# Cross attention 0: the negated maxima put into the score banks by VectorE in place of a second pair of matmuls

## The chip, the cores and the metric

One core of one Trainium2 chip runs the whole program: a stack of twelve layers over 1024 tokens of width 128. The metric is device time in microseconds (us) of one execution. The kernel before takes 5865.0 us (median of 3 runs, 5858.02 to 5866.67). Only the second layer, cross attention 0, is changed, apart from two constants that nothing used.

## The reference

The layer computes, for 16 heads of size 64, with 1024 queries from the layer's normalised input and about 6,400 keys from a shared context (51 tiles of 128 keys):

```
qw = (q_in @ Wq + bq).reshape(B, M, HEADS, QSIZE)
kw = (k_in @ Wk + bk).reshape(B, N, HEADS, QSIZE)
vw = (v_in @ Wv + bv).reshape(B, N, HEADS, KSIZE)
a = jnp.einsum('bmhd,bnhd->bhmn', qw, kw) / jnp.sqrt(jnp.float32(QSIZE))
a = jnp.where(key_mask[:, None, None, :], a, -jnp.inf)
a = jax.nn.softmax(a, axis=-1)
o = jnp.einsum('bhmn,bnhd->bmhd', a, vw).reshape(B, M, HEADS * KSIZE)
return o @ Wo + bo
```

The softmax takes off a maximum for each query and head before the exponential. Any number near the true maximum will do, as long as it is the same for all keys of that query.

## The kernel before

The 16 heads are taken as 8 pairs (`P`); one head of a pair lies on partitions 0 to 63, the other on 64 to 127. The keys come in 13 chunks of up to 512 (`C`), that is 51 tiles of 128 keys (`KT`); the last chunk has 3 tiles, and its maxima are 260 keys wide. The program is a list of turns `g`; a turn has 4 steps `s` (3 where the chunk scored has 3 tiles). In turn `g` the approximate maxima of chunk `g` are found, and 14 turns later (`LAG = C + 1`) the exact scores of the same chunk are made, chunk `j = g - LAG`. So in the long middle of the layer, turns 14 to 103, every step holds one key tile of scores and two of the eight maxima (`q`) of a later chunk; the last pair's scores have no maxima beside them.

The order on each engine is written out by hand. A step on TensorE: bf16 maxima `q` (line 2310) into banks 4 and 5; scores of query half 0 into banks 0 and 1; scores of half 1 into banks 2 and 3; the second maxima; the products of the previous tile's probabilities with the values (line 2342). In step 0 of a turn the keys and values of the next chunk (lines 2349 and 2354) come between, and that step's second maxima go to bank 0 instead of bank 4. Once a pair each, in other steps: the queries (line 2360), the rows (line 2368, which turn the maxima found by VectorE into a row for each query), the sums (line 2377), the output (line 2384). `take_banks` makes TensorE wait until whoever read a bank last is done.

Scores of one half are two float32 matmuls, one a head (line 2323, 64 partitions of keys against 512 queries), and two bf16 matmuls of a tile of ones with `Qa`, the negated maxima (line 2325), added on in the same banks:

```
nc.tensor.matmul(ps[:, 2 * half + a, :], lhsT=Kr[...], rhs=Q[...], start=True, stop=False)
mm = nc.tensor.matmul(ps[:, 2 * half + a, :], lhsT=ones[head(a), :], rhs=Qa[...], start=False, stop=True)
```

ScalarE takes the exponential of each half (line 2433) and copies keys, values and rows out of PSUM. GpSimd adds the probabilities of all tiles up for the softmax sums (lines 2579 and 2588), one addition for each half; its sums hold back ScalarE, which has four buffers of probabilities. VectorE takes the maximum of each block of maxima scores (line 2521), in turn order: two a step. It also does, once a pair, eight reciprocals (2508), a product (2537), the query scaling (2528), the residual addition (2543) and, at the end of a turn with `g % C == 12`, the small steps from maxima to rows (2561 to 2564). No DMA runs in this stretch.

Of the kernel before, what the change touches and what calls it, by code (L numbers as in the profile page):

```python
# [16 lines left out]
D = 128  # L17
# [2200 lines left out]
def cross_0(k, io, X, stack):  # L2218
# [17 lines left out]
    folding, copied, folded = k("folding", "maxima_copied", "maxima_folded")  # L2236
# [8 lines left out]
    Qa, ones = k.tile(stack, "Qa", [128, 2, S], BF16), k.tile(stack, "ones", [128, 128], BF16)  # L2245
# [7 lines left out]
    mz = k.tile(stack, "mz", [128, 8, 2, 64], BF16)  # L2253
# [22 lines left out]
    def others_at(g, s):  # L2276
        return [(item, p) for item, p in ((item, pair_for(g, s, turn, step)) for item, turn, step in
                (("queries", -1, 1), ("rows", C, 1), ("sums", LAG + C, 1), ("output", LAG + C + 2, 2))) if p is not None]
# [9 lines left out]
    def pair_for(g, s, turn, step):  # L2288

        p = (g - turn) // C  # L2290
        return p if s == step and (g - turn) % C == 0 and 0 <= p < P else None

    def pe():
# [8 lines left out]
        def maxima(i, s, steps, q):  # L2302
            b = maxima_bank(i, s, steps, q)
            take_banks(b, taken_off(i, q))
            if q == 0:
                nc.tensor.wait_ge(*key_copied.at(i + 1))
                nc.tensor.wait_ge(*query_copied.at(i // C + 1))
            n = ctx.keys_in(i % C)
            for a in range(2):
                mm = nc.tensor.matmul(ps[:, b + a, 0:n], lhsT=Qb[head(a), i // C % 2, q * 128:(q + 1) * 128], rhs=Kb[head(a), i % 2, 0:n], start=True, stop=True)  # L2310
            mm.then_inc(*maxima_mm.up())

        def scores(j, s, half):
            t, p = KT * (j // C) + TPC * (j % C) + s, j // C
            if s == 0 and half == 0:
                nc.tensor.wait_ge(*key_set.at(j + 1))
                if j % C == 0:
                    nc.tensor.wait_ge(*query_set.at(p + 1))
                    nc.tensor.wait_ge(*rows_set.at(p + 1))
# [25 lines left out]
        def keys_and_values(i, j):  # L2345
            take_banks(4, *([key_copied.at(i + 1)] if i < N else []), *([value_set.at(j + 1)] if 0 <= j < N else []))
            if i < N:
                p, c = i // C, i % C
                nc.tensor.matmul(ps[:, 4, :], lhsT=wk[:, p * 128:(p + 1) * 128], rhs=masked[:, c * CHUNK:(c + 1) * CHUNK], start=True, stop=True).then_inc(*key_mm.up())
            if 0 <= j < N:  # L2350
# [12 lines left out]
        def rows(p):  # L2363
            take_banks(4, rows_set.at(p + 1))
            nc.tensor.wait_ge(*rows_step.at(3 * p + 3))
# [21 lines left out]
        nc.tensor.wait_ge(*zeroed.at(2))  # L2387
# [6 lines left out]
        for g, j, steps in turns():  # L2394
            for s in range(steps):
# [3 lines left out]
                last = [q for q in items[1:] if g >= LAG and maxima_bank(g, s, steps, q) == 0]  # L2399
# [10 lines left out]
                if s == 0:  # L2410
                    keys_and_values(g + 1, j + 1)
                elif not others and g >= LAG:
                    for q in between:
                        maxima(g, s, steps, q)
                for item, p in others:
                    {"queries": queries, "rows": rows, "sums": sums, "output": output}[item](p)
                for q in last:
                    maxima(g, s, steps, q)
                if 0 <= j and 0 < t <= KT * P and (j < N or s == 0):
                    products(t - 1)  # L2420

    def act():
# [14 lines left out]
        for g, j, steps in turns():  # L2437
            for s in range(steps):
# [31 lines left out]
                p = pair_for(g, s, C, 1)  # L2470
                if p is not None:
                    nc.scalar.wait_ge(*rows_mm.at(p + 1))
                    if p >= 2:
                        nc.scalar.wait_ge(*scored.at(2 * KT * (p - 1)))
                    nc.scalar.copy(Qa[:, p % 2, :], pair).then_inc(*rows_set.up())
                p = pair_for(g, s, LAG + C, 1)
                if p is not None:
# [3 lines left out]
                    nc.scalar.copy(over[:], pair).then_inc(*sums_set.up())  # L2481

    def dve():
        nc.vector.memset(ones[:], 1.0)
        nc.vector.memset(ones_f[:], 1.0)
        nc.vector.memset(zero_row[:], 0.0).then_inc(*zeroed.up())
        nc.vector.memset(mz[:], 0.0).then_inc(*zeroed.up())
# [21 lines left out]

        for g, j, steps in turns():  # L2510
            for s in range(steps):
                for q in maxima_at(g, s, steps):
                    if g < C and q in by_act:
                        waiting.append((g, q))
                        if len(waiting) > 2:
                            fold(*waiting.pop(0))
                        continue
                    nc.vector.wait_ge(*maxima_mm.at(8 * g + q + 1))
                    if g >= 2 * C and g % C == 0 and q == 0:
                        nc.vector.wait_ge(*rows_step.at(3 * (g // C) - 4))  # L2520
                    nc.vector.tensor_reduce(red[:, g // C % 2, q, :, g % C], ps[:, maxima_bank(g, s, steps, q):maxima_bank(g, s, steps, q) + 2, 0:ctx.keys_in(g % C)], AX, ALU.max).then_inc(*reduced.up())  # L2521
                p = pair_for(g, s, -1, 1)
                if p is not None:
# [4 lines left out]
                    nc.vector.tensor_scalar(Q[:, p % 3, :], both.rearrange("p a n -> p (a n)"), bq[:, p:p + 1], scale, ALU.add, ALU.mult).then_inc(*query_set.up())  # L2528
                for n in range(8):
# [8 lines left out]
                p = pair_for(g, s, LAG + C + 2, 2)  # L2538
                if p is not None:
                    nc.vector.wait_ge(*out_mm.at(p + 1))  # L2540
                    if p:
                        nc.vector.wait_ge(*x_added.at(p))
                        nc.vector.tensor_tensor(X[:], X[:], both.rearrange("p a n -> p (a n)"), ALU.add).then_inc(*x_added.up())
                    else:
                        nc.vector.wait_ge(*constant_set.at(1))
                        nc.vector.scalar_tensor_tensor(X[:], both.rearrange("p a n -> p (a n)"), out_bias[:, 0:1], X[:], ALU.add, ALU.add).then_inc(*x_added.up())
            if 0 <= g < N and g % C == C - 1:
# [10 lines left out]
                if p:  # L2558
                    nc.vector.wait_ge(*rows_step.at(3 * p))
                    nc.vector.wait_ge(*rows_mm.at(p))  # L2560
# [815 lines left out]
class Constants:  # L3376
    def __init__(self, k, stack):
# [4 lines left out]
        self.zero = k.tile(stack, "zero", [1, HALF])  # L3382
        self.roots = k.tile(stack, "roots", [128, 8])
        self.ones, self.ones_col, self.ones16 = k.tile(stack, "ones", [1, 128]), k.tile(stack, "ones_col", [128, 1]), k.tile(stack, "ones16", [128, 16])
        self.ident16, self.below16 = k.tile(stack, "ident16", [128, 128], BF16), k.tile(stack, "below16", [128, 128], BF16)
        self.causal, self.below = k.tile(stack, "causal", [128, 128]), k.tile(stack, "below", [128, 128])
        for t, value in ((self.mean, 1.0 / D), (self.eps, LN_EPS), (self.one_eps, 1.0 + 1e-6), (self.zero, 0.0),
                         (self.ones, 1.0), (self.ones_col, 1.0), (self.ones16, 1.0)):
            nc.vector.memset(t[:], value)
        nc.gpsimd.memset(self.ident[:], 0.0)  # L3390
        nc.gpsimd.memset(self.causal[:], 1.0)
# [4 lines left out]
        nc.gpsimd.affine_select(out=self.causal[:], in_=self.causal[:], compare_op=ALU.is_ge, fill=0.0, base=0,  # L3396
                                pattern=[[1, 128]], channel_multiplier=-1)
# [147 lines left out]
```

## Time and profile before

| | |
|---|---|
| median of 3 runs | 5865.0 us |
| the profiled execution: span | 5863.6 us |
| its own time beside the span | none is shown apart from the span |
| busy in the span: TensorE, VectorE, ScalarE, GpSimd | 5274.1, 2726.8, 3176.0, 2218.6 us |
| the changed layer, first to last exponential | 410.3 to 2503.1 us |
| exponentials in it (line 2433) | 816 of 1114 ns |

A line of a view names the source line, the engine, the operation, its output and input, and how often. Busy times of TensorE are of pipelined matmuls: the distance between the starts of two of them says more than the length of one. In a timeline the bracket gives the idle time before an instruction and what ended it.

### The profile page before, as it was taken

To read this page: it belongs to the slowest core of one execution; us is meant where nothing else is said; L and a number is where in the kernel's file an instruction comes from. 1 tells how busy PE (TensorE), PEld (TensorE's weight loads), DVE (VectorE), ACT (ScalarE), POOL (GpSimd) and SP (SyncE) were. 2 spreads that over 40 slices of the span, in tenths; PEclk is the share of its full clock that TensorE was granted. 3 is DMA by queue.
4 is the path that set the end of the run, shared out by engine and by line. 5 is a ranking of instruction groups with operands and counts; after the bars stand their busy time and mean duration, and the time that the engine had idled before them with its cause. 6 is when DMAs were issued, how large, how long until landed. Compare 5 with 4: busy or idle time off the path is not lost. (4 is left out here: it accounts for less than half of the span.)

```text
span 5863.6 us, 69367 instructions
## 1 busy us (share of the span) xinstructions
PE 5274.1 (90%) x28014; PEld 1717.5 (29%) x28014; DVE 2726.8 (47%) x3143; ACT 3176.0 (54%) x3203; POOL 2218.6 (38%) x1113
## 2 busy tenths in 40 slices
PE   8879999999999999989999689999886788888889
PEld 3213333333333333332243311111342111111123
DVE  5664545454545552015541400000246998898713
ACT  4455555555555555521122399999124677777761
POOL 1119898989888899915533000000000000000000
PEclk8869999999999999989999799999896799999999
DMA  1000000000000000010000120000203000000010
GB/s 50 15 1 1 1 1 1 1 1 1 1 1 1 1 1 1 1 41 1 2 1 4 52 84 11 20 11 2 80 25 123 13 11 11 11 11 11 7 46 31
DMA packets 64433, 100.77 MB, mean 17 GB/s; under 512 B 9846, under 2 KB 49880, under 8 KB 62000
## 3 DMA queue, kind: packets, MB, share of 16 engines
q1 hardware_dynamic: 63906, 95.50, 4.9%
q8 instruction: 222, 3.64, 0.3%
q14 instruction: 99, 0.81, 0.0%
q10 hardware_dynamic: 206, 0.83, 0.0%
HBM read 70.85 MB, written 25.31 MB: 16 GB/s over the span
## 5 line engine op out<-in xcount | busy, mean ns | idle before, releaser
L2433 ACT ACTIVATE Pr<-ps,key_bias 128x1024 f32<-128x1024 f32 x816 | 893.2, 1114 | 1015.4 <-PE ps L2325 1015.4
L2521 DVE TENSOR_REDUCE red<-ps 128x2 f32<-128x1024 f32 (+1 forms) x767 | 908.1, 1185 | 959.2 <-PE ps L2310 954.0
L2579 POOL TENSOR_TENSOR Ps<-Ps,Pr 128x1024 f32<-128x1024 f32 x400 | 944.3, 2361 | 215.9 <-ACT Pr L2433 215.9
L2588 POOL TENSOR_TENSOR Ps<-Ps,Pr 128x1024 f32<-128x1024 f32 x400 | 947.5, 2369 | 0.0
L3206 DVE TENSOR_REDUCE red<-ps 128x1 f32<-128x512 f32 (+3 forms) x1024 | 877.7, 908 | 94.0 <-PE ps L3079 74.7
L3162 ACT ACTIVATE Pr<-ps 128x1024 f32<-128x1024 f32 x816 | 786.2, 1021 | 228.5 <-PE ps L3089 227.9
L2323 PE MATMUL ps<-Q,Kr 64*128 64x512 f32 x3264 | 842.3, 594 | 0.5 <-DVE red L2521 0.2
L2342 PE MATMUL ps<-Pr,Vc 128*64 128x512 f32 x3264 | 790.1, 605 | 0.0
L3336 ACT ACTIVATE Pr<-ps 128x2048 f32<-128x2048 f32 x467 | 726.2, 2024 | 1.6 <-PE ps L3299 1.6
L3079 PE MATMUL ps<-Kp,Q 52*128 52x512 bf16 (+1 forms) x1664 | 441.8, 411 | 172.1 <-DVE red L3206 125.7
L544 POOL IOTA number<- 128x8 f32 x1 | 0.1, 139 | 1157.5 <-POOLq L89 1157.5
L3102 PE MATMUL ps<-Pr,V 128*9 128x512 f32 x3264 | 437.1, 607 | 0.0
L3312 PE MATMUL ps<-Pr,V 128*8 128x512 f32 x3264 | 427.1, 595 | 0.0
L3089 PE MATMUL ps<-Q,Kp 52*128 52x512 bf16 x1632 | 363.8, 387 | 12.2 <-ACT Pr L3162 8.6
L2323 PEld LDWEIGHTS ps<-Q,Kr 64*128 64x128 f32 x3264 | 308.1, 189 | 198.0 <-issue 158.9
L2310 PE MATMUL ps<-Kb,Qb 64*128 64x512 bf16 (+1 forms) x1664 | 326.1, 398 | 40.8 <-DVE red L2521 12.1
L3299 PE MATMUL ps<-Q,Kp 48*128 48x512 bf16 x1632 | 283.8, 385 | 68.6 <-ACT Pr L3336 55.1
L3345 DVE COPY Oc<-ps 128x512 f32<-128x512 f32 x8 | 5.5, 692 | 726.4 <-PE ps L3312 726.4
L3079 PEld LDWEIGHTS ps<-Kp,Q 52*128 52x128 bf16 x1664 | 105.8, 95 | 731.5 <-DVE red L3206 650.6
L2325 PE MATMUL ps<-Qa,ones 64*128 64x512 bf16 x1632 | 310.8, 377 | 0.0
L2342 PEld LDWEIGHTS ps<-Pr,Vc 128*64 128x64 f32 x3264 | 198.0, 136 | 385.1 <-issue 302.9
L1667 POOL IOTA number<- 128x16 f32 x1 | 0.1, 146 | 735.3 <-POOLq L89 735.3
(580 smaller groups left out, 5197.2 us busy)
## 6 DMA issues: line engine op xcount, KB each, us to landing
L_dram_K<-parts SPq DMA_DIRECT2D x26, 384.0 KB, 3.1
Kp<-L_dram_K SPq DMA_DIRECT2D x14, 624.0 KB
L_dram_K<-parts SPq DMA_DIRECT2D x26, 256.0 KB, 2.9
wB<-L_ffn_shares SPq DMA_DIRECT2D x1, 6144.0 KB
w<-L_ffn_experts_w_dram SPq DMA_DIRECT2D x24, 256.0 KB
Kp<-L_dram_K SPq DMA_DIRECT2D x14, 416.0 KB
wB<-L_ffn_shares SPq DMA_DIRECT2D x1, 3584.0 KB, 12.4
ctx<-ctx_dram SPq DMA_DIRECT2D x13, 256.0 KB, 7.4
```

Source lines behind the costliest of these rows:

```text
L2323: nc.tensor.matmul(ps[:, 2 * half + a, :], lhsT=Kr[head(a), j % 16, s * 128:(s + 1) * 128], rhs=Q[head(a), p % 3, sl], start=True, stop=False)
L2342: mm = nc.tensor.matmul(ps[head(a), 6 + half, :], lhsT=Vc[:, j % 3, at:at + 64], rhs=Pr[:, t % 4, half, a, :], start=False, stop=True, ski ...
L2433: nc.scalar.activation(Pr[:, t % 4, half].rearrange("p a n -> p (a n)"), ps[:, 2 * half:2 * half + 2, :].rearrange("p a n -> p (a n)"), AC ...
L2521: nc.vector.tensor_reduce(red[:, g // C % 2, q, :, g % C], ps[:, maxima_bank(g, s, steps, q):maxima_bank(g, s, steps, q) + 2, 0:ctx.keys_i ...
L2579: nc.gpsimd.tensor_tensor(into, into, src, ALU.add).then_inc(*summed0.up())
L2588: nc.gpsimd.tensor_tensor(into, into, src, ALU.add).then_inc(*summed1.up())
L3079: mm = nc.tensor.matmul(ps[:, b + item - first, 0:keys], lhsT=Q[head(a), p, q * 128:(q + 1) * 128], rhs=Kp[head(a), p % 3, at:at + keys], ...
L3102: mm = nc.tensor.matmul(ps[at:at + 9, 6, :], lhsT=A.V[:, kt, 2 * p + a, :], rhs=Pr[:, t % 4, half, a, :], start=False, stop=True, skip_gro ...
L3162: nc.scalar.activation(Pr[:, t % 4, half].rearrange("p a n -> p (a n)"), ps[:, 2 * half:2 * half + 2, :].rearrange("p a n -> p (a n)"), AC ...
L3206: nc.vector.tensor_reduce(red[:, z, first:first + n, g % C], ps[:, b:b + n, 0:ctx.keys_in(g % C)], AX, ALU.max).then_inc(*reduced.up())
L3312: mm = nc.tensor.matmul(ps[at:at + 8, 7, :], lhsT=A.V[:, kt, 2 * p + a, :], rhs=Pr[:, i % 21, :], start=False, stop=True, skip_group_check ...
L3336: nc.scalar.activation(Pr[:, slot:slot + n, :].rearrange("p a n -> p (a n)"), ps[:, bank:bank + n, :].rearrange("p a n -> p (a n)"), ACT.S ...
```

## The change

VectorE now copies the negated maxima into the score banks itself, before the scores of a tile: two copies a tile (128 x 1024, bf16 in SBUF to float32 in PSUM), one for each half. The score matmuls are then issued with `start=False`, so that they add to what lies there, and the matmuls with ones go. For this the negated maxima must stand on every one of the 128 partitions, so `mz` becomes 128 columns wide, the rows are made in two parts in two steps, and ScalarE copies two of 128 x 1024 where it copied one. The list of tiles that ScalarE would preset (`act_seeds`) is empty. On VectorE a step now is: maxima that are not `last`, queries, output addition, the `last` maxima, the two copies for the next tile, then reciprocals. Values come after the last maxima on TensorE instead of before. Maxima outside bank 4 are always written 512 wide.

```diff
+    dve_seeds = [(t, half) for t in range(P * KT) for half in range(2)]
+    act_seeds = [(t, 0) for t in range(P * KT) if (t, 0) not in dve_seeds]
...
+    def seed(engine, copy, t, half, signal):
...
+        if t:
+            engine.wait_ge(*exp_done.at(2 * (t - 1) + half + 1))
+        if t % KT == 0:
+            engine.wait_ge(*rows_set.at(2 * p + 2))
+        copy(ps[:, 2 * half:2 * half + 2, :], seeds[:, p % 2, half]).then_inc(*signal.up())
...
-            take_banks(2 * half, exp_done.at(2 * t + half + 1))
+            nc.tensor.wait_ge(*seeded(t, half))
+            taken[2 * half] = [exp_done.at(2 * t + half + 1)]
...
-                nc.tensor.matmul(ps[:, 2 * half + a, :], lhsT=Kr[head(a), j % 16, s * 128:(s + 1) * 128], rhs=Q[head(a), p % 3, sl], start=True, stop=False)
-            for a in range(2):
-                mm = nc.tensor.matmul(ps[:, 2 * half + a, :], lhsT=ones[head(a), :], rhs=Qa[head(a), p % 2, sl], start=False, stop=True)
+                mm = nc.tensor.matmul(ps[:, 2 * half + a, :], lhsT=Kr[head(a), j % 16, s * 128:(s + 1) * 128], rhs=Q[head(a), p % 3, sl], start=False, stop=True, skip_group_check=True)
...
-            for q in range(8):
-                for a in range(2):
-                    mm = nc.tensor.matmul(ps[head(a), 4 + q // 4, (q % 4) * 128:(q % 4 + 1) * 128], lhsT=mz[:, q, a, :], rhs=k.consts.ident16[:], start=True, stop=True)
+            for a in range(2):
+                for q in range(4):
+                    mm = nc.tensor.matmul(ps[:, 4 + a, q * 128:(q + 1) * 128], lhsT=mz[:, 4 * half + q, a, :], rhs=k.consts.ident16[:], start=True, stop=True)
...
+                        nc.scalar.copy(seeds[:, p % 2, half], ps[:, 4:6, :]).then_inc(*rows_set.up())
...
+                for q in last:
+                    largest(g, s, steps, q)
...
+                            elif half == 0 and last:
+                                nc.vector.wait_ge(*taken_off(g, last[-1]))
+                            seed(nc.vector, nc.vector.tensor_copy, after, half, seeded_by_dve)
...
-                nc.vector.tensor_reduce(mz[:, :, :, 0], red[:, p % 2], AX, ALU.max, negate=True).then_inc(*rows_step.up())
-                nc.vector.wait_ge(*rows_step.at(3 * p + 2))
-                nc.vector.tensor_tensor(mz[:, :, :, 1], neg[:], mz[:, :, :, 0], ALU.subtract).then_inc(*rows_step.up())
+                nc.vector.wait_ge(*rows_step.at(2 * p + 1))
+                nc.vector.tensor_copy(mz[:].rearrange("p q a n -> p (q a) n"), neg[:].rearrange("p q a -> p (q a)").unsqueeze(2).to_broadcast([128, 16, 128])).then_inc(*rows_step.up())
```

## Rows read from the trace of the kernel before

**Rows 1.** Windows: length; PE, PEld, DVE, ACT, POOL busy; clock; DMA
```profile
410.00:2260.00 1850.00, 1840.05 (x9604) 683.39 (x9602) 926.81 (x806) 941.95 (x995) 1633.04 (x714) 1.00 0.00 1
2282.00:2505.00 223.00, 223.00 (x1084) 79.33 (x1084) 10.76 (x10) 114.20 (x110) 221.06 (x96) 1.00 0.00 1
```
**Rows 2.** Timeline of TensorE: a step 0 of a turn, then an ordinary step
```profile
1542.42 0.39 PE L2310 MATMUL ps<-Kb,Qb 64*128 64x512 bf16 x2
1542.64 1.02 PE L2323 MATMUL ps<-Q,Kr 64*128 64x512 f32 x4
1543.50 0.38 PE L2325 MATMUL ps<-Qa,ones 64*128 64x512 bf16 x2
1543.72 1.02 PE L2323 MATMUL ps<-Q,Kr 64*128 64x512 f32 x4
...
1544.89 1.12 PE L2349 MATMUL ps<-ctx_masked,Wk 128*128 128x512 f32 x2
1545.85 1.05 PE L2354 MATMUL ps<-Wv,ctx 128*128 128x128 f32 x8
1546.84 0.39 PE L2310 MATMUL ps<-Kb,Qb 64*128 64x512 bf16 x2
...
1549.02 0.39 PE L2310 MATMUL ps<-Kb,Qb 64*128 64x512 bf16 x2
...
1553.58 0.39 PE L2310 MATMUL ps<-Kb,Qb 64*128 64x512 bf16 x2
```
**Rows 3.** Timeline of VectorE: the last reduction of that step 0
```profile
1547.27 1.23 DVE L2521 TENSOR_REDUCE red<-ps 128x2 f32<-128x1024 f32 x1 [3.19 <-PE ps L2310]
```
**Rows 4.** Timeline of VectorE: a reduction with a ready instruction behind it
```profile
1492.59 1.23 DVE L2521 TENSOR_REDUCE red<-ps 128x2 f32<-128x1024 f32 x1 [1.14 <-PE ps L2310]
1493.73 0.94 DVE L2508 RECIPROCAL over<-over 128x128 f32<-128x128 f32 x1
```
**Rows 5.** Timeline of all engines around one output step: VectorE, GpSimd, TensorE
```profile
1530.33 0.39 PE L2310 MATMUL ps<-Kb,Qb 64*128 64x512 bf16 x2
...
1530.69 1.23 DVE L2537 TENSOR_TENSOR Ur<-Ur,over 128x1024 f32<-128x1024 f32 x1
1530.79 3.34 POOL L2588 TENSOR_TENSOR Ps<-Ps,Pr 128x1024 f32<-128x1024 f32 x1
...
1536.40 2.35 POOL L2588 TENSOR_TENSOR Ps<-Ps,Pr 128x1024 f32<-128x1024 f32 x1
1536.60 1.21 DVE L2543 TENSOR_TENSOR X<-X,ps 128x1024 f32<-128x1024 f32 x1
...
1537.87 0.39 PE L2310 MATMUL ps<-Kb,Qb 64*128 64x512 bf16 x2 [0.58 <-DVE X L2543]
```
**Rows 6.** Groups of VectorE instructions in the whole span, shapes kept apart
```profile
L2528 DVE TENSOR_SCALAR Q<-ps,bq 128x1024 f32<-128x1024 f32 x8 | 10.2, 1278 | 10.8 <-PE ps L2360 10.8
...
L3228 DVE TENSOR_TENSOR mz<-neg,mz 128x16 bf16<-128x16 f32 x8 | 1.4, 180 | 0.3
...
L2743 DVE CAST qparts<-Qf 128x1024 bf16<-128x1024 f32 x2 | 1.4, 694 | 0.1
```
**Rows 7.** Groups of VectorE instructions from 480 to 2280 us
```profile
L2564 DVE TENSOR_TENSOR mz<-neg,mz 128x16 bf16<-128x16 f32 x7 | 9.5, 1355 | 0.2
```
**Rows 8.** Timeline of TensorE: the turn with the rows, steps 1 and 2
```profile
1464.76 0.39 PE L2310 MATMUL ps<-Kb,Qb 64*128 64x512 bf16 x2
...
1468.19 0.64 PE L2368 MATMUL ps<-ident,mz 128*64 128x128 bf16 x16 [0.25 <-DVE red L2521]
...
1470.95 0.39 PE L2310 MATMUL ps<-Kb,Qb 64*128 64x512 bf16 x2
...
1475.82 0.39 PE L2310 MATMUL ps<-Kb,Qb 64*128 64x512 bf16 x2
```
**Rows 9.** Windows in cross attention 3, columns as in rows 1
```profile
4550.00:4700.00 150.00, 109.03 (x687) 21.90 (x685) 138.09 (x176) 102.93 (x109) 0.00 (x0) 0.78 0.03 11
4700.00:5000.00 300.00, 261.99 (x1874) 53.98 (x1871) 269.04 (x328) 225.63 (x234) 0.00 (x0) 0.98 0.03 11
```

More of the change, by code:

```diff
@@ L2244, in cross_0 @@
     Q, Qb = k.tile(stack, "Q", [128, 3, S]), k.tile(stack, "Qb", [128, 2, S], BF16)
-    Qa, ones = k.tile(stack, "Qa", [128, 2, S], BF16), k.tile(stack, "ones", [128, 128], BF16)
+    seeds = k.tile(stack, "seeds", [128, 2, 2, 2, HALF], BF16)
     by_act = (0, 2, 4, 5, 7)
@@ L2277, in others_at @@
         return [(item, p) for item, p in ((item, pair_for(g, s, turn, step)) for item, turn, step in
-                (("queries", -1, 1), ("rows", C, 1), ("sums", LAG + C, 1), ("output", LAG + C + 2, 2))) if p is not None]
+                (("queries", -1, 1), ("first_rows", C, 1), ("second_rows", C, 2), ("sums", LAG + C, 1), ("output", LAG + C + 2, 2))) if p is not None]
     def maxima_bank(g, s, steps, q):
@@ L2291, in pair_for, with behind, seeded @@
         return p if s == step and (g - turn) % C == 0 and 0 <= p < P else None
+    def behind(g, s, steps):
+        return [q for q in list(maxima_at(g, s, steps))[1:] if g >= LAG and maxima_bank(g, s, steps, q) == 0]
+    tile_turns = {KT * (j // C) + TPC * (j % C) + s: (g, s, steps) for g, j, steps in turns() for s in range(steps) if 0 <= j < N}
+    dve_seeds = [(t, half) for t in range(P * KT) for half in range(2)]
+    act_seeds = [(t, 0) for t in range(P * KT) if (t, 0) not in dve_seeds]
+    def seeded(t, half):
+        return seeded_by_dve.at(dve_seeds.index((t, half)) + 1) if (t, half) in dve_seeds else seeded_by_act.at(act_seeds.index((t, half)) + 1)
+    def seed(engine, copy, t, half, signal):
+        p = t // KT
+        if t:
[3 more added lines that the diff above has]
+        copy(ps[:, 2 * half:2 * half + 2, :], seeds[:, p % 2, half]).then_inc(*signal.up())
     def pe():
@@ L2398, in pe @@
                 others = others_at(g, s)
-                last = [q for q in items[1:] if g >= LAG and maxima_bank(g, s, steps, q) == 0]
+                last = behind(g, s, steps)
                 between = [q for q in items[1:] if q not in last]
@@ L2415, in pe @@
                 for item, p in others:
-                    {"queries": queries, "rows": rows, "sums": sums, "output": output}[item](p)
+                    if item in ("first_rows", "second_rows"):
+                        rows(p, ("first_rows", "second_rows").index(item))
+                    else:
+                        {"queries": queries, "sums": sums, "output": output}[item](p)
                 for q in last:
                     maxima(g, s, steps, q)
+                if s == 0:
+                    values(j + 1)
                 if 0 <= j and 0 < t <= KT * P and (j < N or s == 0):
@@ L2469, in act @@
                     nc.scalar.copy(Ur[:], ps[:, 6:8, :].rearrange("p a n -> p (a n)")).then_inc(*acc_copied.up())
[L2470 to L2475, printed above, removed]
+                for half in range(2):
+                    p = pair_for(g, s, C, 1 + half)
+                    if p is not None:
+                        nc.scalar.wait_ge(*rows_mm.at(2 * p + half + 1))
+                        if p >= 2:
+                            nc.scalar.wait_ge(*scored.at(2 * KT * (p - 1)))
+                        nc.scalar.copy(seeds[:, p % 2, half], ps[:, 4:6, :]).then_inc(*rows_set.up())
                 p = pair_for(g, s, LAG + C, 1)
@@ L2508, in inverse, with largest @@
             nc.vector.reciprocal(over[:, sl], over[:, sl]).then_inc(*inverse_step.up())
+        def largest(g, s, steps, q):
+            if g < C and q in by_act:
+                waiting.append((g, q))
+                if len(waiting) > 2:
+                    fold(*waiting.pop(0))
+                return
+            nc.vector.wait_ge(*maxima_mm.at(8 * g + q + 1))
+            if g >= 2 * C and g % C == 0 and q == 0:
+                nc.vector.wait_ge(*rows_step.at(2 * (g // C) - 3))
+            nc.vector.tensor_reduce(red[:, g // C % 2, q, :, g % C], ps[:, maxima_bank(g, s, steps, q):maxima_bank(g, s, steps, q) + 2, 0:ctx.keys_in(g % C)], AX, ALU.max).then_inc(*reduced.up())
         for g, j, steps in turns():
             for s in range(steps):
+                last = behind(g, s, steps)
                 for q in maxima_at(g, s, steps):
[L2513 to L2521, printed above, removed]
+                    if q not in last:
+                        largest(g, s, steps, q)
                 p = pair_for(g, s, -1, 1)
@@ L2528, in dve @@
                     nc.vector.tensor_scalar(Q[:, p % 3, :], both.rearrange("p a n -> p (a n)"), bq[:, p:p + 1], scale, ALU.add, ALU.mult).then_inc(*query_set.up())
+                p = pair_for(g, s, LAG + C + 2, 2)
+                if p is not None:
+                    nc.vector.wait_ge(*out_mm.at(p + 1))
+                    if p:
+                        nc.vector.wait_ge(*x_added.at(p))
+                        nc.vector.tensor_tensor(X[:], X[:], both.rearrange("p a n -> p (a n)"), ALU.add).then_inc(*x_added.up())
+                    else:
+                        nc.vector.wait_ge(*constant_set.at(1))
+                        nc.vector.scalar_tensor_tensor(X[:], both.rearrange("p a n -> p (a n)"), out_bias[:, 0:1], X[:], ALU.add, ALU.add).then_inc(*x_added.up())
+                for q in last:
+                    largest(g, s, steps, q)
+                t = KT * (j // C) + TPC * (j % C) + s
+                if 0 <= j < N or (j == -1 and s == steps - 1):
+                    for half in range(2):
+                        after = t + 1 if j >= 0 else 0
+                        if (after, half) in dve_seeds:
+                            if after == 0:
+                                for q in range(8):
+                                    nc.vector.wait_ge(*taken_off(g, q))
+                            elif half == 0 and last:
+                                nc.vector.wait_ge(*taken_off(g, last[-1]))
+                            seed(nc.vector, nc.vector.tensor_copy, after, half, seeded_by_dve)
                 for n in range(8):
```

50 lines of the change are left out of this document (19 added, 31 removed).

## The prediction

> **What bounds it now.** I read the windows first, then the timelines of TensorE, VectorE and GpSimd in the stretch that is changed, and last the prices of VectorE's instructions. From 410 to 2260 us, where every step holds scores of one pair and maxima of the next, TensorE is busy 1840 of 1850 us at a granted clock of 1.00, its 2.4 GHz level; VectorE is busy 927 us, half of the time, ScalarE 942 and GpSimd 1633 [rows 1]. So TensorE is the bound and GpSimd stands close behind it. From 2282 to 2505 us, the last pair's scores with no maxima, GpSimd is busy 221 of 223 us [rows 1]: there it is as much the bound as TensorE.
>
> The reader should see the step in TensorE's timeline [rows 2]. An ordinary step runs from 1549.02 to 1553.58, 4.56 us; step 0 of a turn, with the next chunk's keys and values, from 1542.42 to 1549.02, 6.60 us. A turn of four is 6.60 + 3 x 4.56 = 20.28 us. Scores of a half start 0.86 us ahead of the ones matmuls (1542.64 to 1543.50), and those 0.22 us ahead of the next (1543.50 to 1543.72). Maxima are 0.22 us to the next instruction and 0.39 us to their end. VectorE starts on them 0.04 us later (1546.84 + 0.39 = 1547.23, start 1547.27) [rows 2, 3]. TensorE starts 0.06 us after VectorE ends (1536.60 + 1.21 = 1537.81, start 1537.87) [rows 5].
>
> **What goes.** Two ones pairs a tile, 2 x 0.22 = 0.44 us of TensorE: 4.12 us for an ordinary step, 6.16 for step 0. Over 51 tiles and 8 pairs that would be 180 us. It is the whole gain there can be, and only if nothing else takes the bound. GpSimd's two additions a tile of 2.35 us [rows 5] already ask for 4.70 us, more than 4.12, so for a start a turn cannot be below 4 x 4.70 = 18.8 us.
>
> **What comes: two copies a tile on VectorE.** No row has VectorE writing PSUM. From the dear side: all its 1024-wide instructions on float32 with PSUM as source take 1.21 to 1.28 us, the reduction 1.23 [rows 3, 5, 6]. From the cheap side: a cast of the same width within SBUF takes 0.69 us, two elements at a time [rows 6]. I take the reduction's price, for the copy too has float32 in PSUM on one side. An instruction that is ready starts 0.09 us before the one ahead of it ends (1492.59 + 1.14 = 1493.73) [rows 4]. So a copy costs VectorE 1.14 us, with ends of 0.60 and 1.19.
>
> **The new ordinary step, from VectorE's queue.** Its order is reduction 0, reduction 1, copy 0, copy 1 for the next tile. Reduction 1 can't be ready when reduction 0 ends: both maxima use banks 4 and 5, and TensorE may write the second only when the first is read. Put reduction 0 at 0. It ends at 1.23; TensorE starts the second maxima at 1.29 and ends at 1.68; reduction 1 starts at 1.72, copy 0 at 2.86, copy 1 at 4.00, the next reduction 0 at 5.14. The rest fits within: copy 0 ends at 4.09, scores run from 4.15, the second half waits for copy 1 until 5.29 and is issued by 6.15, before the next reduction 0 ends at 6.37. The exponential of half 0 ends about 6.3, ahead of the next copy 0 at 8.0. So VectorE is the bound: 5.14 us in place of 4.56, +0.58. In four instructions of 1.14 to 1.23 us and one hole of 0.49 us there is no slack left, and TensorE waits about a fifth of the step.
>
> **Step 0.** Keys wait for reduction 0: 1.23 + 0.06, then 0.96 us to the last maxima (1544.89 to 1545.85 is the keys' place [rows 2]), 0.39 + 0.04, so the last reduction starts at 2.68. Copy 0 waits for its end (1.23 + 0.06): 3.97, and two copies end the step at 6.25, against 6.60: -0.35. Values, which now come after these maxima, lie in TensorE's slack.
>
> **Steps with other work.** The rows are made in two steps now. The first took 1470.95 - 1464.76 = 6.19 us, the second 4.87 (to 1475.82) [rows 8]. Both now hold three reductions with a rows block (0.64 us [rows 8]) between: 1.23 + 0.49 + 1.23 + 0.06 + 0.64 + 0.39 + 0.04 = 4.08, then 1.23 + 0.04 and 2.28 for the copies, 7.63. That is +1.4 and +2.8. The steps with queries, sums and output (7.54 us before [rows 5]) already have VectorE in the chain; I leave them even, with -0.35 and +0.58 as ends from the steps above. ScalarE's second rows copy lies in its idle half.
>
> **Work that was free.** Once a pair VectorE does eight reciprocals of 0.94 us [rows 4], the product of 1.23 us [rows 5] and the new copy that fills `mz` (128 x 2048; twice a cast, 1.4, to twice a reduction, 2.5, which I take). These stood in VectorE's idle half and stand in its chain now: 7.5 + 1.2 + 2.5 = 11.2 us. A small instruction on two SBUF inputs took 0.18 us alone and 1.36 us beside GpSimd [rows 6, 7]: the `mz` copy may meet the same wait of 1.2 us.
>
> **The sum.** For each pair: 33 ordinary steps x 0.58 = 19.1; 13 steps 0 x -0.35 = -4.6; rows 4.2; freed work 11.2; together +29.9 us. The stretch holds 90 turns of 13, 6.92 pairs: +207. One pair's reciprocals and product fall behind it: -9. So +198 us. In the last pair nothing is gained: GpSimd keeps its 4.70 us a tile, and VectorE has room. The first maxima, before 410 us, and the two constants at the start change nothing that a later engine waits for. The profiled execution has a span of 5863.6 us, 1.4 below the median of 5865.0. 5863.6 + 198 + 1.4 = **6063 us**.
>
> Everything hangs on the copy. There are 90 x 51/13 x 2 = 706 of them in the stretch, so each 0.01 us is 7 us. At 0.86 us a copy the change would be even; at 1.19 it is +35 more; at 1.04, 70 less. The forecast's own range is 5990 to 6110.
>
> **Rivals.** *The copies run two elements at a time (faster).* At 0.60 us VectorE's step is 1.72 + 1.14 + 1.20 = 4.06, under TensorE's 4.12; GpSimd's 18.8 us a turn becomes the bound, -1.5 on 88 turns' worth (90 less the short ones), -132; half of the 11.2 us freed work gives back 39. About 5770 us. It decides below 0.86 us a copy. For it speaks the cast of 0.69 us; against it, that this cast has SBUF on both sides, while every 1024-wide row with PSUM is over 1.2 us. The Trainium skill's page "VectorE: DVE Perf Modes" (the perf-mode tier table) lists a copy with PSUM on a side as up to two a cycle; the same page (Mode 2x_1P) asks for 16 bits on every tensor, which a float32 bank isn't. By the table alone the result would be this rival's. Chance 0.10.
>
> *The copies block GpSimd.* When VectorE multiplied two SBUF tensors, GpSimd's addition beside it took 3.34 us in place of 2.35 [rows 5]. If each copy did this, additions and copies would take turns: 4.70 + 2.28 = 6.98 us a tile, 2848 us for 408 tiles in place of the 2095 from 410 to 2505: about 6620. Against it: the residual addition at 1536.60, with one input in SBUF and one in PSUM, left the GpSimd addition that it ran beside at 2.35 us [rows 5]. The Trainium skill's page "SBUF — State Buffer" (SBUF: two separate sides) tells of an exclusive lock for two-port modes or two SBUF inputs, and the 3.34 us agrees. Chance 0.04.
>
> *TensorE's clock falls.* Its work would be 18.52 us of a turn of 21.7, 85%. In cross attention 3 a window with TensorE busy 87% kept 0.98, one with 73% had 0.78 [rows 9]. At 0.78 a turn needs 23.7 us: +3.5 x 88 = +305, about 6170. The share is nearer to the first window. Chance 0.05.
>
> *The copies cost about 0.86 us*, between the two ends, and it comes out even: about 5865 us, chance 0.03.
>
> If the bank overwrote the preset instead of adding to it, the instructions and the time would be the same.
>
> **How the numbers follow.** Forecast 0.78, with blocked GpSimd 0.04 and the lower clock 0.05 slower too: slower 0.87, same 0.03, faster 0.10. A measurement of this kernel can tell about 0.2%, 12 us, from no change. For 8 in 10 the range takes the forecast's whole own range and goes on to a copy of about 0.98 us below and to the clock case's 6170 above: 5950 to 6170.
>
> **What would show it.** In the changed profile: copies of about 1.2 us on VectorE; VectorE busy over 90% from 410 to the end of the maxima; ordinary steps of 5.1 us with TensorE waiting 0.3 to 0.5 us for a copy before each half; a hole of about 0.5 us between the two reductions; GpSimd at 2.35 us with idle time before it. Copies of 0.7 us, or steps under 4.6 us, would make it wrong; so would GpSimd's additions over 3 us, or a granted clock below 0.95.

## The result, and the profile after

The changed kernel takes 6076.0 us (median of 4 runs, 6071.03 to 6079.74) against 5862.57 (4 runs, with one more of the kernel before): a ratio of 1.0365, 95% interval 1.0352 to 1.0378, slower by 213 us. The forecast was 6063, the range 5950 to 6170. The profiled execution has a span of 6078.0 us.

First the page of the changed kernel: busy times of the whole program, and the groups that answer to the changed lines.

```profile
PE 5313.5 (87%) x26382; PEld 1620.8 (27%) x26382; DVE 3645.5 (60%) x3947; ACT 3194.5 (53%) x3211; POOL 2230.6 (37%) x1111
...
L2547 DVE TENSOR_REDUCE red<-ps 128x2 f32<-128x1024 f32 (+1 forms) x767 | 902.9, 1178 | 345.0 <-PE ps L2331 344.9
L2624 POOL TENSOR_TENSOR Ps<-Ps,Pr 128x1024 f32<-128x1024 f32 x400 | 955.7, 2389 | 403.7 <-ACT Pr L2459 402.9
L2312 DVE CAST ps<-seeds 128x1024 f32<-128x1024 bf16 x816 | 959.2, 1220 | 96.9 <-ACT Pr L2459 88.3
L2344 PE MATMUL ps<-Q,Kr 64*128 64x512 f32 x3264 | 870.6, 628 | 91.6 <-DVE ps L2312 91.4
```

The 816 copies take 1220 ns each, 959 us of VectorE that were not there before; VectorE's busy time went up by 919 (3645.5 less 2726.8). TensorE's scores now wait for the copies (91.4 us of idle time before them), and GpSimd, at 2.36 to 2.39 us an addition, waits for exponentials.

The windows of the stretch with maxima, and of the last pair (columns as in [rows 1]):

```profile
410.00:2475.00 2065.00, 1901.12 (x8246) 603.82 (x8246) 1715.02 (x1511) 968.00 (x1008) 1657.63 (x718) 0.99 0.00 1
2500.00:2720.00 220.00, 196.51 (x834) 62.55 (x830) 125.07 (x99) 104.95 (x104) 210.15 (x92) 0.97 0.00 1
```

VectorE went from half of the time to 83% (1715 of 2065); TensorE from 99% to 92%. In the last pair GpSimd is still the bound, but it is busy 210 of 220 us where it was busy 221 of 223. The change splits by two ends, that of the last maxima and that of GpSimd's last addition; here they are, first before, then after:

```profile
2256.77 0.70 DVE L2521 TENSOR_REDUCE red<-ps 128x2 f32<-128x520 f32 x1 [1.56 <-PE ps L2310]
2512.38 2.34 POOL L2588 TENSOR_TENSOR Ps<-Ps,Pr 128x1024 f32<-128x1024 f32 x1
...
2459.41 0.70 DVE L2547 TENSOR_REDUCE red<-ps 128x2 f32<-128x520 f32 x1 [0.73 <-PE ps L2331]
2523.26 10.58 DVE L2592 TENSOR_TENSOR Ur<-Ur,over 128x1024 f32<-128x1024 f32 x1
2542.62 2.37 POOL L2624 TENSOR_TENSOR Ps<-Ps,Pr 128x1024 f32<-128x1024 f32 x1 [9.85 <-ACT Pr L2459]
2725.13 2.41 POOL L2633 TENSOR_TENSOR Ps<-Ps,Pr 128x1024 f32<-128x1024 f32 x1
```

The last maxima ended at 2257.5 us before and at 2460.1 after, +202.6. The last addition ended at 2514.7 and at 2727.5, +212.8: the stretch with maxima holds 203 us of the change and the last pair the other 10. Those 10 are one hole of GpSimd, 9.85 us. VectorE's product there took 10.58 us in place of 1.22: behind the addition that it met, four more ran without a gap, and the product ended 1.07 us after the last of them. The copies for the next tile stood behind it in VectorE's queue, so scores, exponentials and then GpSimd itself ran out of work.

VectorE's timeline of a step 0 and an ordinary step, and the starts that bound the parts of one pair:

```profile
1300.06 1.22 DVE L2547 TENSOR_REDUCE red<-ps 128x2 f32<-128x1024 f32 x1
...
1371.22 1.22 DVE L2547 TENSOR_REDUCE red<-ps 128x2 f32<-128x1024 f32 x1
1373.98 1.23 DVE L2547 TENSOR_REDUCE red<-ps 128x2 f32<-128x1024 f32 x1 [1.54 <-PE ps L2331]
...
1377.50 1.22 DVE L2547 TENSOR_REDUCE red<-ps 128x2 f32<-128x1024 f32 x1
1379.21 1.23 DVE L2547 TENSOR_REDUCE red<-ps 128x2 f32<-128x1024 f32 x1 [0.49 <-PE ps L2331]
1380.35 2.34 DVE L2312 CAST ps<-seeds 128x1024 f32<-128x1024 bf16 x2
1382.60 1.22 DVE L2547 TENSOR_REDUCE red<-ps 128x2 f32<-128x1024 f32 x1
...
1543.86 0.69 DVE L2547 TENSOR_REDUCE red<-ps 128x2 f32<-128x520 f32 x1
...
1599.26 1.22 DVE L2547 TENSOR_REDUCE red<-ps 128x2 f32<-128x1024 f32 x1
```

Steps are counted here from first reduction to first reduction, as the prediction counted them. The ordinary step is 5.10 us (1382.60 - 1377.50) and step 0 is 6.28. Only one gap is left in the ordinary step, the 0.49 us in which TensorE makes the second maxima. TensorE's side of it:

```profile
1381.62 2.25 PE L2344 MATMUL ps<-Q,Kr 64*128 64x512 f32 x8 [0.27 <-DVE ps L2312]
```

TensorE waits 0.27 us for the copy of half 0; the wait for that of half 1 is hidden in the eight scores, which last 2.25 us where unhindered ones last 1.88.

One cycle of 51 steps, by the starts above (before: the same parts by the starts of the steps in TensorE's timeline, shown here, 267.82 us from one sums step to the next). The last column is the prediction's terms, put to the parts in which they lie; by rounding they make 30.0 where it had 29.9:

```profile
1214.92 0.39 PE L2310 MATMUL ps<-Kb,Qb 64*128 64x512 bf16 x2
1274.60 0.39 PE L2310 MATMUL ps<-Kb,Qb 64*128 64x512 bf16 x2
1436.73 0.28 PE L2310 MATMUL ps<-Kb,Qb 64*128 64x260 bf16 x2
1458.15 0.39 PE L2310 MATMUL ps<-Kb,Qb 64*128 64x512 bf16 x2
1482.74 0.39 PE L2310 MATMUL ps<-Kb,Qb 64*128 64x512 bf16 x2
```

| part of a pair | steps | before | after | change | predicted |
|---|---|---|---|---|---|
| sums to output, with reciprocals and product | 11 | 59.68 | 71.16 | +11.5 | +12.1 |
| eight plain turns | 32 | 162.13 | 172.64 | +10.5 | +11.1 |
| turn with short maxima, query, fill of `mz` | 4 | 21.42 | 25.14 | +3.7 | +3.3 |
| turn with the rows, and the next step 0 | 4 | 24.59 | 30.26 | +5.7 | +3.5 |
| together | 51 | 267.82 | 299.20 | +31.4 | +30.0 |

The one part that is well off is the turn with the rows. The timelines of VectorE and GpSimd there:

```profile
1565.64 2.35 POOL L2633 TENSOR_TENSOR Ps<-Ps,Pr 128x1024 f32<-128x1024 f32 x1
1566.30 2.78 DVE L2609 CAST mz<-neg 128x2048 bf16<-128x2048 f32 x1
1567.94 3.33 POOL L2624 TENSOR_TENSOR Ps<-Ps,Pr 128x1024 f32<-128x1024 f32 x1
1569.00 1.21 DVE L2547 TENSOR_REDUCE red<-ps 128x2 f32<-128x1024 f32 x1
...
1577.97 1.23 DVE L2547 TENSOR_REDUCE red<-ps 128x2 f32<-128x1024 f32 x1 [1.44 <-PE ps L2331]
...
1585.48 1.22 DVE L2547 TENSOR_REDUCE red<-ps 128x2 f32<-128x1024 f32 x1
```

TensorE's timeline beside it:

```profile
1570.27 2.08 PE L2368 MATMUL ps<-ctx_masked,Wk 128*128 128x512 f32 x2 [3.09 <-DVE red L2547]
```

The windows of the same place, columns as in [rows 1], the clock behind the busy times:

```profile
1562.00:1570.20 8.20, 5.17 (x24) 1.36 (x22) 7.43 (x7) 4.19 (x4) 8.20 (x4) 0.97 0.01 3
1570.20:1577.50 7.30, 7.24 (x20) 3.07 (x20) 3.59 (x4) 1.85 (x3) 3.38 (x2) 0.56 0.00 0
```

The fill of `mz` (2.78 us) stands in front of the next reduction; TensorE waits 3.09 us for that, and then, after a window at 0.97, runs 7 us at a granted clock of 0.56, close to its 1.2 GHz level: the keys take 2.08 us where they take 1.12 [rows 2]. This step 0 is 8.97 us instead of 6.28. In the stretch's six cycles it was 7.6 twice and 8.7 to 9.0 four times.

### The profile page after: what moved, and what is told of

It reads as the page before. It is cut to its first block and busy times, and to the rows that moved or that the text cites. A ratio compares the mean times of both kernels' runs of the same rounds, so it can differ in the third digit from the quotient of the medians.

```text
span 6078.0 us, 67056 instructions
## 1 busy us (share of the span) xinstructions
PE 5313.5 (87%) x26382; PEld 1620.8 (27%) x26382; DVE 3645.5 (60%) x3947; ACT 3194.5 (53%) x3211; POOL 2230.6 (37%) x1111
## 5 line engine op out<-in xcount | busy, mean ns | idle before, releaser
L2312 DVE CAST ps<-seeds 128x1024 f32<-128x1024 bf16 x816 | 959.2, 1220 | 96.9 <-ACT Pr L2459 88.3
L2344 PE MATMUL ps<-Q,Kr 64*128 64x512 f32 x3264 | 870.6, 628 | 91.6 <-DVE ps L2312 91.4
L2344 PEld LDWEIGHTS ps<-Q,Kr 64*128 64x128 f32 x3264 | 265.1, 186 | 487.7 <-DVE ps L2312 400.6
```

Of the source, the lines that this page charges most:

```text
L2312: copy(ps[:, 2 * half:2 * half + 2, :], seeds[:, p % 2, half]).then_inc(*signal.up())
L2344: mm = nc.tensor.matmul(ps[:, 2 * half + a, :], lhsT=Kr[head(a), j % 16, s * 128:(s + 1) * 128], rhs=Q[head(a), p % 3, sl], start=False, s ...
```

## The experiments

**Half 0 by ScalarE.** One copy of the two goes to an engine that was busy under half of the time.

```diff
-    dve_seeds = [(t, half) for t in range(P * KT) for half in range(2)]
+    dve_seeds = [(t, half) for t in range(P * KT) for half in range(2) if half or t == 0]
...
                 if 0 <= j < N and (t + 1, 0) in act_seeds:
+                    for q in behind(g, s, steps)[-1:]:
+                        nc.scalar.wait_ge(*taken_off(g, q))
                     seed(nc.scalar, nc.scalar.copy, t + 1, 0, seeded_by_act)
```

> ScalarE makes the copy for half 0 (all tiles but the first), VectorE keeps half 1. Theory (VectorE's queue is the bound): a step on VectorE falls from 5.1 to 1.72 + 1.14 + 1.11 = 3.97 us, under TensorE's 4.12; GpSimd's two additions of 2.36 us bound the step instead, about 18.8 us a turn against 20.28 before, so about 5730 to 5800 us, faster than both kernels. Rival (the hand-over is the bound: exponential, then copy, then scores on the same banks, whoever copies): steps stay at 5 us or more and the time above 5950 us.

Measured: 5870.7 us, ratio 1.0007 (0.9998 to 1.0017): the whole loss is gone, and nothing is won. VectorE's queue was the cause of the loss, but its relief is not worth what I expected. By TensorE's steps, the eight plain turns take 154.0 us where they took 162.1, but sums to output take 65.45 (59.68 before) and the turn with the rows, with the step 0 behind it, 27.1 (24.6): these give 8 us back. The last pair, from the end of the last maxima to that of GpSimd's last addition, takes 277 us where it took 257. An ordinary step is 4.12 to 4.27 us, not 4.12 throughout. ScalarE's timeline (its copy has no bracket: it is ready as soon as the exponentials are through):

```profile
1400.57 2.12 ACT L2459 ACTIVATE Pr<-ps,key_bias 128x1024 f32<-128x1024 f32 x2 [1.23 <-PE ps L2344]
...
1402.58 1.02 ACT L2312 CAST ps<-seeds 128x1024 f32<-128x1024 bf16 x1
```

Scores, two exponentials, copy, scores: a ring through ScalarE has taken the place of VectorE's queue. That is read from the timeline, not shown by a run; and GpSimd is close behind, busy 147.6 of the 154.0 us of the eight plain turns. The fill of `mz` on VectorE, between two additions of GpSimd:

```profile
1462.22 2.37 POOL L2626 TENSOR_TENSOR Ps<-Ps,Pr 128x1024 f32<-128x1024 f32 x1
1464.36 1.31 DVE L2611 CAST mz<-neg 128x2048 bf16<-128x2048 f32 x1
1464.54 3.33 POOL L2635 TENSOR_TENSOR Ps<-Ps,Pr 128x1024 f32<-128x1024 f32 x1
```

It takes 1.31 us here and 2.78 in the changed kernel (2.87 on average), and in both it ends 1.08 or 1.09 us after the addition that it met. Here it started 0.23 us before that addition ended; in the changed kernel, with 1565.64 + 2.35 = 1567.99 as the end, 1.69 us before. So the difference is a wait for GpSimd, and the next addition waits in its turn: 3.33 us in both.

**Copy 0 between the reductions.** VectorE's order becomes reduction, copy 0, reduction, copy 1 wherever both maxima use bank 4.

```diff
+                    if n == 0 and early:
+                        seed(nc.vector, nc.vector.tensor_copy, KT * (j // C) + TPC * (j % C) + s + 1, 0, seeded_by_dve)
```

> VectorE's order in steps without work for bank 0 is reduction, copy 0, reduction, copy 1, so that copy 0 fills the hole in which VectorE waits for the second maxima. Theory: the ordinary step falls from about 5.1 to 4 x 1.13 = 4.55 us; 33 x 6.92 such steps save about 0.5 us each, 115 us: 5940 to 5980 us. Rival (hand-over): copy 0 is no earlier than its exponential allows and nothing is gained, 6060 to 6090 us.

Measured: 6023.93 us, ratio 1.0268 (1.0251 to 1.0285): -52 us, short of the theory's 96 to 136. The hole can be filled, but not wholly won: the ordinary step is 4.86 us, four instructions of 1.13 us and a new wait of 0.25 us, of copy 1 for an exponential; a plain turn of four steps takes 21.16 us where it took 21.59. VectorE's timeline:

```profile
1400.59 1.22 DVE L2547 TENSOR_REDUCE red<-ps 128x2 f32<-128x1024 f32 x1
1401.72 1.22 DVE L2312 CAST ps<-seeds 128x1024 f32<-128x1024 bf16 x1
...
1404.31 1.23 DVE L2312 CAST ps<-seeds 128x1024 f32<-128x1024 bf16 x1 [0.25 <-ACT Pr L2459]
1405.45 1.22 DVE L2547 TENSOR_REDUCE red<-ps 128x2 f32<-128x1024 f32 x1
```

**No copies at all.** Neither copies nor ones matmuls, so the kernel leaves out taking the maxima off: the floor.

```diff
-            nc.tensor.wait_ge(*seeded(t, half))
-            taken[2 * half] = [exp_done.at(2 * t + half + 1)]
+            take_banks(2 * half, exp_done.at(2 * t + half + 1))
...
-                mm = nc.tensor.matmul(..., start=False, stop=True, skip_group_check=True)
+                mm = nc.tensor.matmul(..., start=True, stop=True)
...
-                        if (after, half) in dve_seeds:
+                        if False and (after, half) in dve_seeds:
```

> No copies at all and no ones matmuls: the scores start fresh, so the maxima are not taken off (left out of the computation). Theory: TensorE's ordinary step is 4.12 us and GpSimd's 4.7 bounds the stretch, so 5710 to 5790 us, the whole gain that the removal of the matmuls can give. Rival (the ones matmuls were hidden, so nothing was to be gained): 5850 to 5880 us.

Measured: 5752.6 us, ratio 0.981 (0.9793 to 0.9826), as expected. All that the ones matmuls can give is 110 us of the 180 that their time adds up to. The ordinary step is 4.12 us, the prediction's figure for TensorE without them, and step 0 is 6.38 (6.16). The window, columns as in [rows 1]:

```profile
480.00:2200.00 1720.00, 1692.79 (x8091) 602.27 (x8087) 913.01 (x779) 921.09 (x988) 1621.41 (x706) 1.00 0.00 1
```

TensorE is busy 98%, GpSimd 94%: so the second bound, GpSimd, is near. The copies themselves cost 6076 - 5753 = 323 us.

**The copy of half 1 twice.** The measured price of one more copy in VectorE's queue.

```diff
+        if half:
+            copy(ps[:, 2 * half:2 * half + 2, :], seeds[:, p % 2, half]).then_inc(*doubled.up())
+            engine.wait_ge(*doubled.at(t + 1))
```

> VectorE makes the copy for half 1 twice. Theory: every step of the stretch with maxima grows by one more copy, 1.2 us with the wait for the first: 353 tiles x 1.2 = +420 us, 6450 to 6530 us, and the last pair, bound by GpSimd, hardly grows. Rival (VectorE has slack that a wait elsewhere covers): less than half of that, under 6290 us.

Measured: 6575.3 us, ratio 1.1211: +499, where 374 to 454 was expected. VectorE's timeline (1404.77 copy 0, 1405.91 the extra copy, 1407.16 copy 1) shows the copy and the wait for its end at 1.25 us from start to start:

```profile
1404.77 1.23 DVE L2315 CAST ps<-seeds 128x1024 f32<-128x1024 bf16 x1
1405.91 1.22 DVE L2313 CAST ps<-seeds 128x1024 f32<-128x1024 bf16 x1
1407.16 1.23 DVE L2315 CAST ps<-seeds 128x1024 f32<-128x1024 bf16 x1
```

1.25 us for 353 tiles is 441. The rest is some 58 us, and half of it can be placed. By TensorE's steps a plain turn is 26.63 us where the clock holds, 5.04 more than in the changed kernel, four times 1.26. In many turns a single step of 6.36 us took 7.83 or 7.84, and there the clock is low:

```profile
1382.80:1390.60 7.80, 6.28 (x22) 1.49 (x20) 6.47 (x7) 2.23 (x2) 5.71 (x3) 0.78 0.01 2
```

Such turns make the plain ones together 30 us longer; the other 28 us, in the turns with other work, are not worked out. What VectorE is given, the kernel pays in full.

**The fill of `mz` by ScalarE.** The work that made the slow step goes to ScalarE, busy under half of the time.

```diff
-                nc.vector.wait_ge(*rows_step.at(2 * p + 1))
-                nc.vector.tensor_copy(mz[:]..., neg[:]...to_broadcast([128, 16, 128])).then_inc(*rows_step.up())
...
+                nc.scalar.copy(mz[:]..., neg[:]...to_broadcast([128, 16, 128])).then_inc(*rows_step.up())
```

> The changed kernel, with the copy that fills mz moved from VectorE to ScalarE. In the changed kernel step 0 of the rows turn takes 12.75 us: VectorE's mz copy of 2.8 us (with a wait for GpSimd's port) keeps TensorE waiting 3.1 us, and behind it TensorE runs some 7 us at a granted clock of 0.56. Theory: without this copy in VectorE's queue the wait and the fall of the clock both go, step 0 takes 7.3 to 8.3 us, and 7 pairs save 5 us each: 6030 to 6055 us. Rival (the wait for the keys' bank makes that step long, not the copy): step 0 stays near 12.7 us and the time at 6070 to 6082 us.

Measured: 6045.59 us, ratio 1.031 (1.0294 to 1.0326), as expected: -30 us, 4.4 a pair. By TensorE's starts, with the fill in it, the step 0 of 12.75 us takes 7.75. Counted from first reduction to first reduction, the step behind the fill takes 7.04 or 7.05 us in all six cycles, where it was 7.6 to 9.0. TensorE's wait for the reduction is 0.27 us in place of 3.09 and the granted clock behind it 1.00, so the long wait and the low clock came from this one instruction. What is left over an ordinary step 0 (6.28) stands beside a wait of 0.69 us, for an exponential that ScalarE starts after its fill of 1.90 us.

**ScalarE's half 0, eased.** With the fill by ScalarE, its copy ahead of its copy of the sums, and the output one step later, a version to beat both kernels (of the diff only the output's line is shown):

```diff
-                (..., ("output", LAG + C + 2, 2)))
+                (..., ("output", LAG + C + 2, 3)))
```

> ScalarE copies half 0 as in the first experiment, and besides fills mz, makes its copy for the next tile ahead of its copy of the sums, and the output comes one step later. Theory: the first experiment's regular turns are faster than before (19.25 against 20.27 us), and the gain is given back in the steps of sums (8.6), output (11.1) and rows (7.8 us); eased, these give back about 6 us a pair, 40 us: 5815 to 5850 us, faster than before. Rival (those steps wait for work that only moves, VectorE's reciprocals): 5855 us or more.

Measured: 5866.45 us, ratio 1.0001 (0.9992 to 1.001). The time is the rival's; the work had only moved. Three ordinary steps with a reciprocal take 4.78 us, where those without take 4.12 to 4.27, and the step with the product takes 8.24. The timeline of VectorE, GpSimd and TensorE in the step with the product:

```profile
1253.73 2.62 DVE L2600 TENSOR_TENSOR Ur<-Ur,over 128x1024 f32<-128x1024 f32 x1
1255.23 3.32 POOL L2630 TENSOR_TENSOR Ps<-Ps,Pr 128x1024 f32<-128x1024 f32 x1
...
1257.55 0.39 PE L2331 MATMUL ps<-Kb,Qb 64*128 64x512 bf16 x2 [3.06 <-DVE red L2555]
1257.87 2.68 PE L2361 MATMUL ps<-Pr,Vc 128*64 128x512 f32 x8
```

VectorE's product of two SBUF tensors waits for the addition before, and the addition shown waits for the product; a reduction waits behind it, TensorE for that, 3.06 us, and the products behind take 2.68 instead of 1.94 us. In the last pair the same product takes 10.72 us.

**Copy between the exponentials.** The version just shown, with ScalarE's copy ahead of its second exponential.

```diff
+                    if early and (t + 1, 0) in act_seeds:
+                        seed(nc.scalar, nc.scalar.copy, t + 1, 0, seeded_by_act)
```

> As the eased version, and in ordinary steps ScalarE's copy of half 0 stands between the two exponentials. Theory: in the first experiment the ordinary step of 4.26 us is the chain scores, two exponentials, copy (1.06 + 1.10 + 1.10 + 1.02); with the copy ahead of the second exponential it is 3.2 us and TensorE's 4.12 us bounds the step: about 0.3 us a turn, 25 us less than the eased version. Rival (GpSimd's 4.6 us a tile already bounds it): no difference from the eased version, within 8 us.

Measured: 5960.17 us, ratio 1.0161 (1.0148 to 1.0175), a miss by 120 us. One ordinary step in three is 5.02 us and a step 0 is 7.16 (6.6 in the eased version): the second exponential comes 1 us later, VectorE's copy 1 waits for it, TensorE for that, as the timeline shows:

```profile
1404.08 1.23 DVE L2312 CAST ps<-seeds 128x1024 f32<-128x1024 bf16 x1 [0.95 <-ACT Pr L2459]
...
1405.36 1.13 PE L2344 MATMUL ps<-Q,Kr 64*128 64x512 f32 x4 [0.45 <-DVE ps L2312]
```

**The holes filled with the right work.** From the eased version: reciprocals between the two reductions, the product with `Ur` by GpSimd, and ScalarE's copy ahead of its copy of `Ur`.

```diff
                     if q not in last:
                         largest(g, s, steps, q)
+                    while inverses:
+                        inverse(*inverses.pop(0))
...
-                    nc.vector.tensor_tensor(Ur[:], Ur[:], over[:], ALU.mult).then_inc(*inverse_step.up())
+                    nc.gpsimd.tensor_tensor(Ur[:], Ur[:], over[:], ALU.mult).then_inc(*inverse_step.up())
```

> The version with half 0 preset by ScalarE and half 1 by VectorE (fill of mz by ScalarE, output one step later), with three things moved out of VectorE's and ScalarE's chains: the eight reciprocals stand between the two reductions of a step, the product with Ur is made by GpSimd, and ScalarE's copy stands ahead of its copy of Ur in the step where that waits for the products. Theory (three places give time back: the sums step loses TensorE's wait of 1.71 us, six reciprocal steps go from 4.78 to about 4.36 us, and the 3.06 us wait behind the product goes, with the slower matmuls behind it, some 3.5 us together): -7.6 us a pair, 6.9 pairs, -52 us: about 5815 us, 5800 to 5835, ratio 0.989 to 0.995, the first version of this idea that beats the kernel before. Rival (work only moves, as in the version before this one: GpSimd's 2.35 us more, or a hole that is too narrow, comes back as a wait elsewhere): 5850 to 5880. Reciprocal steps of 4.8 us would speak for the rival.

Measured: 5802.52 us, ratio 0.99 (0.9884 to 0.9915): 1% faster than the kernel before, clear of what runs differ by. The reciprocal stands in the hole, and beside GpSimd's product no instruction of VectorE is longer than elsewhere (timeline of VectorE and GpSimd):

```profile
1229.53 1.23 DVE L2560 TENSOR_REDUCE red<-ps 128x2 f32<-128x1024 f32 x1 [0.92 <-PE ps L2331]
...
1230.67 0.94 DVE L2549 RECIPROCAL over<-over 128x128 f32<-128x128 f32 x1
...
1236.20 2.37 POOL L2645 TENSOR_TENSOR Ur<-Ur,over 128x1024 f32<-128x1024 f32 x1
```

Ordinary steps with a reciprocal take 4.12 to 4.27 us, as those without (three had taken 4.78, not six as expected); the sums step went from 9.59 to 7.61, the product's from 8.24 to 4.27, the eleven steps from 65.43 to 56.53 us. The last pair went from 271.8 to 260.4 us, by the ends used above: with the product on GpSimd, VectorE has nothing there that waits for GpSimd. The three moves were not run one by one. Half of what the floor leaves is won: 59 of 110 us.

**The same reciprocals with VectorE's own two copies.** The version with the fill by ScalarE, with only the order of the reciprocals changed:

```diff
                     if q not in last:
                         largest(g, s, steps, q)
+                    while inverses:
+                        inverse(*inverses.pop(0))
```

> The changed kernel with VectorE's copies for both halves, mz filled by ScalarE, and VectorE's eight reciprocals between the two reductions of a step instead of behind the copies. Theory (the 0.49 us between the reductions is a hole that VectorE can't fill with copies of its own order, but can with a reciprocal of 0.85 us from start to start): a step with a reciprocal goes from 5.91 to about 5.5 us, 8 x 0.42 = 3.4 us a pair, 23 us: about 6022 us, 6010 to 6032, against 6046 with the reciprocals behind the copies. Rival (the chain through both reductions and the second maxima is what counts, so that a reciprocal between them delays all behind it by its whole length): 6040 to 6055.

Measured: 6024.32 us, ratio 1.0274 (1.026 to 1.0288), as expected: -21 us against 6045.59. A step with a reciprocal takes 5.31 us where it took 5.91, against 5.10 without.

## Why the prediction was right

**What goes.** Right: 4.12 us of TensorE's work in the ordinary step, as the run without copies shows. The whole gain there was to have is 110 us, not 180. That GpSimd would limit a faster step is half borne out: its additions start 2.31 us apart, so eight of them fill 18.5 of the 18.74 us of a plain turn there (6.38 + 3 x 4.12), where the prediction had 18.8 as the least.

**What comes.** The copy was taken at the reduction's price, 1.14 us from start to start, between 0.60 and 1.19. It measured 1.22 us long and 1.12 to 1.14 from start to start (1404.77 to 1405.91). The Trainium skill's "VectorE: DVE Perf Modes" (What auto-detection actually checks) asks, for two elements at a time, that every tensor have 16 bits, or that the one source and the destination both lie in SBUF. The copy has neither, and 1220 ns for 1024 elements, the price of the reduction, agrees. By the tier table of the same page alone it could have been half, and no run here shows that. The rival of two elements at a time falls with this.

**The steps.** Ordinary 5.10 for 5.14 us, step 0 6.28 for 6.25, rows 7.51 and 7.50 for 7.63 each (1577.97 to 1585.48), the hole of 0.49 us exact. This was the chain through two reductions and TensorE's maxima between them, worked out with two handovers of 0.04 and 0.06 us; VectorE ran it step by step, where TensorE had set the pace before.

**What was free.** Each reciprocal costs 0.81 us (5.91 less 5.10; predicted 0.94), and the fill 2.78 (predicted 2.5, with a possible wait of 1.2 that the sum left out; with nearly no wait it is 1.31, in the changed kernel 2.87 on average: the copy's own price was put too high and the wait left out, and that the two errors cancel is luck). That the turn with the rows cost 2.2 us a pair more than predicted is a step that failed: step 0 there was put at 6.25 like any other, but TensorE waited 3.09 us for the reduction behind the fill, and behind that wait its clock was low. The run with the fill by ScalarE has neither: 7.04 us, in place of 7.6 to 9.0.

**Rivals.** GpSimd was not blocked by the copies: its additions are 2.36 to 2.39 us, with 404 us of idle time before them. What does wait for GpSimd, and makes it wait, is the product and the fill: in the stretch each ends about 1.08 us after the addition that it came in on, and the next addition takes 3.3 us. The Trainium skill's "SBUF — State Buffer" (SBUF: two separate sides) tells of an exclusive lock for two SBUF inputs or two-port modes; the 2.62 us product beside the 3.32 us addition, and the fill, agree, and copies into PSUM don't show it.

The 10.58 us in the last pair are more than one addition's wait: why the product did not get in after the first is open.

The clock did not fall for the stretch as a whole (0.99), but it does so for some 7 us in single places: a rival given a chance of 0.05 for the whole was right in the small.

**The last pair.** This step failed: the prediction left it even, because GpSimd keeps its pace and VectorE has room. It cost 10 us. VectorE's room was taken by a wait, 10.58 us for a product that the sum had put outside the stretch at 1.23, with the copies behind it in the queue. The run with the product on GpSimd bears this out: its last pair is 3 us longer than that of the kernel before (260.4 and 257.3 us), not 10.

**What did not show.** VectorE was not over 90% busy but 83%: it is busy for all but 0.49 us of an ordinary step, 90%, but all but 1.54 of a step 0, 75%, and these were forgotten in that figure. TensorE's wait before half 0, 0.27 us, is a little under the 0.3 to 0.5 named; that for half 1, 2.25 - 1.88 = 0.37 us, is within. Of the 213 us, the stretch to the last maxima holds 203 (predicted 198) and the last pair 10 (predicted 0).

## What to carry to other kernels

Before work goes from a saturated engine to one that is half busy, lay the second engine's instructions of one step end to end with the handovers between: 50% busy was room for 2.3 us, and two copies of 1.1 us plus a hole of 0.5 us overfilled it. Price a new instruction by its nearest row with the same memories on its two sides. Once an engine has become the bound, look for instructions in its queue that others could take, and for the hole that its own dependency leaves: here reordering and moving three small things made 0% into 1%, after a big move alone made nothing. And look in the queue for an instruction that can wait for another engine: all behind it waits too, and here that made the other engine run dry.

## What the runs showed of the hardware

Behind a single TensorE wait of about 3 us came up to 7 us at a granted clock of 0.56, and behind a wait of the same 3.09 us in another cycle only 4 us of slower matmuls; behind a 2.12 us wait before the output the clock was 1.00 once and 0.82 another time. What decides between these was not tried. ScalarE's copy of 128 x 1024 bf16 into a PSUM bank pair took 1.02 us, less than VectorE's 1.22.

VectorE's product of two SBUF tensors took 1.22 us where GpSimd had paused, 2.62 us where it came in 1.54 us before the end of an addition, and 8.4 to 11.5 us in the last pair of seven of the eight versions that have copies and product on VectorE (1.29 in the one with the copy twice). The addition behind it took 3.0 to 3.3 us in place of 2.35. Why the last pair's products waited through several additions was not tried. The same product on GpSimd took 2.37 us and made no instruction of VectorE beside it longer.
